# Fewer idle matrix products at the start, and the last two activations of block 1 in SBUF, in an expert-routed feed-forward kernel

## The reference, cut to what matters

```python
def block1(h, ids, W):             # W = ctx_2048, four experts; gate, up and down use one W
    for e in range(4):
        g = silu(einsum('bsd,fd->bsf', h, W[e])); u = einsum('bsd,fd->bsf', h, W[e])
        out = where(expert(ids) == e, einsum('bsf,df->bsd', g * u, W[e]), out)
def block2(h, Wg, W1, W2, W3):     # eight experts, the best two of each token
    w = softmax over the top 2 of h @ Wg.T, spread to eight columns
    y = sum over e of w[e] * ((silu(h @ W1[e].T) * (h @ W2[e].T)) @ W3[e].T)
x = x + block1(layernorm(x), ids, ctx)
x = x + block2(layernorm(x), Wg, W1, W2, W3)
```

## Time and profile before

| | us |
|---|---|
| Median of three runs | 160.36 (160.21 to 160.94) |
| The profiled execution, its own time | 161.3 |
| Its span, from first to last instruction | 159.5 |
| PE busy in the span | 154.3 |
| DVE, ACT, POOL busy | 97.4, 68.2, 51.7 |

### The profile page before, as it was taken

One profiled execution on the slowest core, in us unless ns is written; L12 is line 12 of the kernel. 1 busy time (PEld: TensorE's weight loads), 2 busy tenths in 40 slices (PEclk: granted clock), 3 DMA queues, 4 the chain that ended last, 5 costly groups with the idle time before them and its releaser, 6 DMA issues.

```text
span 159.5 us, 2464 instructions
## 1 busy us (share of the span) xinstructions
PE 154.3 (97%) x904; PEld 131.6 (83%) x904; DVE 97.4 (61%) x223; ACT 68.2 (43%) x123; POOL 51.7 (32%) x49
## 2 busy tenths in 40 slices
PE   7989999999999999999999999999999999999992
PEld 2367899889899787888889878898888888888891
DVE  0749886763966696477985538717447444444453
ACT  3266958855457623444744522232222222222220
POOL 0665893778839603444742400000000000000000
PEclk9999999999999999999999999999999999999999
DMA  3976173033120200330000000000003000000003
GB/s 98 334 265 199 43 266 101 0 99 102 23 80 10 91 4 0 99 99 0 0 4 0 0 0 2 4 0 0 0 0 136 0 0 0 2 0 4 0 0 132
DMA packets 4620, 8.76 MB, mean 55 GB/s; under 512 B 768, under 2 KB 1408, under 8 KB 4608
## 3 DMA queue, kind: packets, MB, share of 16 engines
q1 hardware_dynamic: 4176, 8.34, 16.6%
q10 hardware_dynamic: 432, 0.27, 0.5%
HBM read 7.55 MB, written 1.05 MB: 54 GB/s over the span
## 4 chain that ended last, share of the span: by engine, by line
PE 89%; DVE 6%; ACT 2%; issue 1%; DVEq 0%
PE z L723 50%; PE y L751 31%; PE z L761 5%; PE y L678 2%; DVE act_lo L581 1%; DVE z L625 1%; DVE x_sb L657 1%; PE y L666 1%; ACT act_hi L404 1%; ACT hT_hi L378 1%; DVE hT_lo L521 1%; DVE top_i L547 0%; DVE gate_rows L570 0%; PE y L695 0%; PE y L691 0%
## 5 line engine op out<-in xcount | busy, mean ns | idle before, releaser
L723 PE MATMUL z<-hT_hi,w_hi 128*128 128x512 f32 x120 | 47.4, 395 | 0.9 <-ACT hT_hi L378 0.5
L723 PE MATMUL z<-hT_hi,w_lo 128*128 128x512 f32 x120 | 47.2, 393 | 0.0
L437 ACT ACTIVATE silu<-z 128x512 f32<-128x512 f32 x38 | 22.8, 600 | 53.1 <-PE z L723 53.1
L751 PE MATMUL y<-w_hi,act_lo 128*128 128x256 f32 x152 | 43.2, 284 | 0.0
L751 PE MATMUL y<-w_hi,act_hi 128*128 128x256 f32 x152 | 43.0, 283 | 0.0
L751 PE MATMUL y<-w_lo,act_hi 128*128 128x256 f32 x152 | 43.0, 283 | 0.0
L723 PE MATMUL z<-hT_lo,w_hi 128*128 128x512 f32 x120 | 37.3, 392 | 0.0
L307 POOL TENSOR_TENSOR w_lo<-raw,w_hi 128x768 fp32r<-128x768 f32 (+1 forms) x15 | 25.4, 1697 | 23.9 <-ACT w_hi L369 23.9
L614 DVE TENSOR_TENSOR z<-gate,z 128x512 f32<-128x512 f32 x23 | 16.0, 695 | 27.4 <-PE z L723 26.8
L751 PEld LDWEIGHTS y<-w_hi,act_lo 128*128 128x128 f32 x152 | 29.0, 191 | 1.3
L751 PEld LDWEIGHTS y<-w_lo,act_hi 128*128 128x128 f32 x152 | 29.0, 191 | 1.2
(11 more groups left out here) (55 smaller groups left out, 96.0 us busy)
## 6 DMA issues: line engine op xcount, KB each, us to landing
raw<-weights_dram SPq DMA_DIRECT2D x11, 384.0 KB, 3.1
raw<-weights_dram SPq DMA_DIRECT2D x8, 256.0 KB, 5.0
x_sb<-x_dram SPq DMA_DIRECT2D x4, 256.0 KB, 4.8
out_dram<-x_sb SPq DMA_DIRECT2D x2, 256.0 KB, 2.6
out_dram<-x_sb SPq DMA_DIRECT2D x2, 128.0 KB, 2.0
out_dram<-x_sb ACTq DMA_DIRECT2D x2, 128.0 KB, 2.1
consts_sb<-consts_dram SPq DMA_DIRECT2D x1, 68.0 KB, 3.8
ids_sb<-token_ids_dram ACTq DMA_DIRECT2D x1, 4.0 KB, 4.0
```

The lines of the kernel that those rows point to most:

```text
L437: nc.scalar.activation(silu[:, q % BUFFERS, :], z_banks(q)[0][:], ACT.Silu).then_inc(silu_done, 1)
L723: return nc.tensor.matmul(bank[:], w[b][:, c, cols], tokens[:, h, k, :], **flags)
L751: last = nc.tensor.matmul(o, a[:, q % BUFFERS, rows], w[b][:, c, wd], start=(first and j == 0), stop=(c == CHUNKS[b] - 1 and j == 2), skip ...
```

## The change

`WARM` is 17 in place of 24, and two more such products stand between the transposes of the first two token tiles and the transposes of the gates. `act_place` gives the SBUF buffer for steps 14 and 15 too, and `up(17)` waits for the activation of step 15 where it waited for its `act_lo`; the wait of `up(16)` stays at `act_lo` of step 13.

```diff
-WARM = 24
+
+WARM, WARM_BETWEEN = 17, 2
...
-            return z_banks(q)[0][:] if STEPS[q][0] == 0 else act[:, q % BUFFERS, :]
+            return z_banks(q)[0][:] if q < FIRST[1, 0] - 2 else act[:, q % BUFFERS, :]
...
                 elif b == 1 and q < FIRST[1, 0] + 2:
 
-                    pe.wait_ge(act_lo_done, 2 * q - FIRST[1, 0] - 2)
+                    if q == FIRST[1, 0]:
+                        pe.wait_ge(act_lo_done, q - 2)
+                    else:
+                        pe.wait_ge(act_done, q - 1)
...
-            def warm():
-
-                for _ in range(WARM):
+            def warm(count):
+
+                for _ in range(count):
                     nc.tensor.matmul(z[3][:], warm_sb[:, 0:P], warm_sb[:], start=True, stop=True)
...
-            warm()
+            warm(WARM)
 
             pe.wait_ge(consts_in, 16)
             transpose_tokens(0, 0, (0, 1))
+            warm(WARM_BETWEEN)
             transpose_gates(0, 0, gate_bank(0, 0))
             transpose_tokens(0, 0, (2, 3))
```

## The result

The changed kernel takes **159.38 us** in the median of nine runs (159.22 to 159.65), the kernel before 160.46 (159.80 to 161.27, nine runs): a ratio of 0.9935, interval 0.9915 to 0.9955, or 1.08 us less. The forecast was 159.1 us and 1.29 us less, in a range (158.5 to 159.8) that held the time. The profiled execution of the changed kernel took 159.55 us, with a span of 157.7.

A forecast was written before the change was run, and what follows sets the result against it. PE bounds the kernel, busy 154.3 of 159.5 us, so time comes only from its work or waits. Gains of 0.71 (start) and 0.58 (border) sum to 1.29 us: 160.36 - 1.29 = 159.1 us, range 158.5 to 159.8.

The forecast's parts named there:

- Part A: Idle products at the start: seven fewer ahead, two added between transposes; 0.71 us gained, bounds -0.43 and 1.09.
- the prediction's own formula: Gain at the start, 1.09 + 0.04 - 0.21k us: 0.92 for k = 1, 0.71 for 2, 0.50 for 3.
- k: Number of idle products by which the pace changes sooner than in the profiled execution before; taken as 2.
- Rival 1: Start: pace changes early (k of 5 or more), norm sets the transposes' start; 159.7 to 160.2 us, chance 0.15.
- Part B: PE's wait at step 17 for act_lo of step 15 goes: 0.61 us gained, 0.58 net of 0.03 costs.
- rival 2: At step 17 another PE wait (low weights or hT) replaces the old one; B is 0, 159.65 us, chance 0.05.
- Rival 3: After the idle products the clock level does not hold, first real products run slowly; 162.5 us, chance 0.05.
- Two of the signs: Expected in the new profile: a span of 157.8 to 158.5 us; 3.25 us from the gates' transposes to down(14).

The follow-up runs named there:

- experiment 1: Changed kernel with only the start changed (17 idle products, 2 between the transposes), activations of steps 14 and 15 back in PSUM: 159.92 us, ratio 0.9959.
- experiment 3: Changed kernel without the two idle products between the transposes (17 ahead, none between): 159.14 us, ratio 0.9901.
- experiments 4 and 6: Changed kernel with step 14's activation back in PSUM: 159.44 us (4); changed kernel with 9 idle products between the transposes in place of 2: 160.90 us (6).
- experiment 7: Changed kernel with 10 idle products ahead of the transposes and none between: 159.89 us, ratio 0.9963.
- experiment 8: Changed kernel with no idle products at all: 160.77 us, ratio 1.0028.

## Why the prediction was right, and where it was off

**What bounds the kernel.** Right: PE, and time came only out of its idle products and its last wait. The 1.2 us of shift from the start reached the border whole.

**Part A** was predicted at 0.71 us and measured 0.60 (experiment 1). The mechanism was the one described, and the rows are close: the second token transposes at 9.00 (9.1 in the text), `up(0)` at 10.14 (10.2). The first transposes, at 7.51, are ahead of the 7.6 to 7.8 of the text, which had them need two `norm` tiles; the first needs one, and as the second waits, little comes of it. That the pace changed two products sooner in the new profile, as I had assumed for the median, is chance. By the prediction's own formula 0.60 lies between k = 2 and k = 3, where I had taken 2; the interval of experiment 1 takes in both. The choice of k was partly luck: the profiled execution of before was an extreme, 161.3 us against timed runs of 159.80 to 161.27, and its 7.12 us is the latest change that can be read in any profile here (the earliest is 4.87). Reading that execution's cost as it stands would have given 1.09 and a median of 158.7. But taking its whole distance of 0.94 us from the median for the pace change would have given 1.13 - 0.94 = 0.19, further from 0.60 than my 0.71. No run shows which k is typical.

**Rival 1**, that `norm` sets the start, was put as an exception for k of 5 or more, with 0.15. It is rather the common case in a weaker form. Of the five profiled executions with 17 products ahead, PE is held by `norm` in three: by the second tile in the changed kernel (pace change at 6.27 us), for 0.3 us in experiment 1 (5.41) and 0.6 in experiment 3 (4.87). In experiments 4 and 6 (both 6.70) it is not held, and starts at 7.60 and 7.58, only 0.1 us later than the changed kernel. So most of the spread in the pace change is swallowed, and the new runs lie within half a microsecond. That the change would narrow the spread follows from the same formula; I did not draw it.

**The rule of the Trainium skill** ("TensorE: Matmul & The Clock Gate", "What's actually happening") that the point of the rise differs from run to run: the traces agree. The pace changed between 4.87 and 7.12 us in the nine executions in which it can be read, with PE's first product at 1.17 or 1.18 us in all.

**Part B** was predicted at 0.58 us, and measured 0.54 in the rows (3.86 - 3.32), 0.55 by span less start, 0.49 in the medians. The 0.03 us that I had charged for the cast and subtraction of step 14 from SBUF are there: the gates' transposes take 0.70 or 0.71 us in the seven profiled executions that have step 14 in SBUF and no wait for `gate_rows`, and 0.67 in the three that have it in PSUM (the kernel before, experiments 1 and 4). What is left of the difference is in the same place: from the first of these transposes to the first product of `up(17)` PE takes 59.47 - 58.99 = 0.48 us, where my terms gave 0.35 (half 1) + 0.07 + 0.03 = 0.45. Nothing new was late behind it, as argued; rival 2 did not happen.

**Rival 3**, the clock, did not happen with 17 products, and experiments 7 and 8 show that with ten idle products or none it does. Its price was too high: I charged up to 17 slow products (3.4 us), and with no idle product at all the kernel loses 160.77 - 159.14 = 1.6 us. In the profiled executions 0.90 us of that is there when `up(0)` starts, behind slow transposes, two slow products add 0.41, later waits take back 0.2, and the border adds the 0.43 that is not the clock's.

In experiment 8 the level rose 0.8 us after PE's first product, with only transposes before it; in the nine executions above it rose 3.7 us or more after a first product (4.87 - 1.17). **The rule of the Trainium skill** ("TensorE: Matmul & The Clock Gate", "Part 4: PE-mode transpose") is that transposes do not count for the clock. By that rule the rise of experiment 8 would have come no sooner behind the first product than elsewhere. The measurement, one execution, speaks against the rule for these float32 transposes.

**The sum.** 1.29 predicted, 1.08 measured: 0.11 of it from A, 0.09 from B, the rest from the rounding of medians. The forecast's own best improvement was missed. The text costs the two products between the transposes at 0.43 us on the path and does not say that this is a loss to be had back; experiment 3 took back 0.24. Two of the signs were a little off: the span is 157.7 us (157.8 to 158.5 in the text), and the stretch at the border 3.32 us (3.25, which left out the 0.03).

## What to carry to other kernels

A profile is one execution. Where its time stands outside the timed runs, find the part that varies, and cost an edit there at the typical value and not at the profiled one. Work that warms an engine up is free only up to the moment when the data arrive: size it so that it ends just before that in the typical execution, keep the pause behind it short, and put none behind the wait. And read a loss where it arises: 0.43 us of what experiments 7 and 8 lost lay not at the start but 30 us later, where two instructions of other engines met that had missed each other. A buffer that a late, low-priority read holds back can be freed by writing the value elsewhere, and then the price is read between two fixed points of the waiting engine, with the same stretch elsewhere as the measure, rather than from the wait's own length (0.36 us here, for a gain of 0.55).

## What the runs showed of the hardware

The column for the granted clock said 1.00 in windows in which the products' spacing shows the 1.2 GHz level, in the stretch before the first rise (in experiment 8 in every window up to 18 us, though the level was low until 11.4). In experiment 7 it showed the fall and the rise after it (0.71, 0.50, 0.50, 0.59 from 8 to 12 us). The spacing of equal products is the better witness: 0.43 us at the low level and 0.217 us at the high one for the idle products of 512 columns, and 0.22 and 0.11 for the transposes.

The level rose between 4.87 and 7.12 us with PE busy from 1.17 us on. It was high behind pauses of 0.6 and 0.7 us. In the profiled execution that paused for 2.0 us it was high behind the pause too and fell 1.0 us later; three of the twelve timed runs of that kernel lost nothing. With no idle products, twelve float32 transposes and two products came before the rise.

A DVE subtraction of 128x16 took 1.30 us in place of 0.23 where it started just behind a POOL product of 1.29 us (experiments 7 and 8, L635).
